# A block elimination for a 34 x 34 set of Fourier frequencies: the turned copy of U by two DMAs, apply two units ahead

## The chip, the cores and the metric

The kernel runs on one NeuronCore of a Trainium2 chip. The metric is the time of one execution on the device in microseconds (us); the value given is the median of three executions. Engines are named PE (TensorE; PEld is its weight load), ACT (ScalarE), DVE (VectorE), POOL (GpSimd) and SP (SyncE); SPq and POOLq are the queues that begin DMAs.

## The reference, cut to what matters

```python
def _L0_conv_ref(x, weight, bias):          # x: (32, 128, 32, 32) after a group norm
    xp = jnp.pad(x, ...)                     # 34 x 34
    xfft = jnp.fft.rfft2(xp, norm='ortho')   # 34 x 18 frequencies
    W = cal_wfft_ortho(weight, n, cout, cin) # one 128 x 128 complex matrix per frequency
    zfft = W @ xfft
    ...
def cal_wfft_ortho(weight, n, cout, cin):
    vfft = jnp.fft.rfft2(weight, s=(n, n), norm='ortho')
    wfft = vH @ vfft + eps * I
    ortho = I - 2.0 * (vfft @ jnp.linalg.solve(wfft, vH))
x = x + _L0_conv_ref(_gn(x), L0_conv_weight, L0_conv_bias)
```

All is float32. The costly part is a 128 x 128 complex Hermitian solve at each of 580 frequencies.

## The kernel before

The frequencies are taken four at a time, as 145 "quads". Each 128 x 128 matrix is split in two halves of 64, and each half is eliminated in blocks of 16 rows, 4 block steps to a half. A matrix half is held in 128 partitions: four quadrants of 32 partitions, a quadrant holding the real and the imaginary part of 16 rows.

The work on the solver is a list of jobs written out by hand in `order()`: form and pre build matrices, mid and final couple the halves, pivot gathers the first pivots, and a **sweep** does one block step for all quads of a group. Group 0 has 82 quads, group 1 has 63, and there are 8 sweeps of each. A sweep is cut into units of 8 quads (some of 6 or 7): 11 units for group 0, 8 for group 1, 152 in all. Each engine runs its own program through the jobs, in order, and waits on semaphores; nothing is reordered. On PE a unit has three parts:

- `apply(u)` (L1040): 32 small products with the factored pivot block `ce`; U comes out in PSUM bank 0. Its stationary operand `ce[h, ..., :, slot + t]` has 32 columns that lie 32 floats apart.
- `turn_u(u)` (L1049): one product with a constant matrix, which makes JU, U times the imaginary unit, in PSUM bank 1.
- `update(u)` (L1063): 32 products of [U, JU] with U. Stationary are 128 columns, moving 64 or 128 columns, read from 32 partitions each.

A float32 product is two instructions in the trace, so 32 products are x64. ACT copies U (L1244, `copy_u`) and JU (L1250, `copy_ju`) into the buffer `u_emb`, and gathers the pivot blocks of the next step for the unit before (L1211, `gather_next`). DVE subtracts the update from the matrices, in four instructions (L1499). The order on PE and the wait that the text below speaks of:

```python
for u in range(lo, hi):                        # L1163
    if u + 1 < hi: apply(u + 1)
    update(u)
    if u + 1 < hi: turn_u(u + 1)
# in update(u):
if u: pe.wait_ge(S["upd_copied"], 2 * u - 1)   # L1057: DVE has done two of its four for u - 1
```

`upd_bank(u, c)` is bank `2 + (4u + c) % 6`: an update takes four of six banks, so it meets the first two banks of the unit before. DVE counts `upd_copied` up after its second and fourth instruction. After a sweep, PE waits in `settle` for all of `upd_copied`. The factoring of a pivot (DVE, to `place`, L1490) runs beside the pre, mid or final job that stands between two sweeps.

## Time and profile before

| | |
|---|---|
| median of 3 runs | 2848.31 us (2847.0, 2848.31, 2858.18) |
| span of the profiled execution | 2851.4 us (its own time is given only by this span) |
| PE busy, DVE busy, ACT busy | 86%, 67%, 49% of the span |
| first and last instruction of `apply` | 541.5 and 2410.1 us |

Shares are averages over all stages. The sweeps lie between 541 and 2418 us, and each is 30 to 50 us long with the other jobs between them.

### The profile page before, as it was taken

To read this page: it belongs to the slowest core of one execution; us is meant where nothing else is said; L and a number is where in the kernel's file an instruction comes from. 1 tells how busy PE (TensorE), PEld (TensorE's weight loads), DVE (VectorE), ACT (ScalarE), POOL (GpSimd) and SP (SyncE) were. 2 spreads that over 40 slices of the span, in tenths; PEclk is the share of its full clock that TensorE was granted. 3 is DMA by queue.
4 is the path that set the end of the run, shared out by engine and by line. 5 is a ranking of instruction groups with operands and counts; after the bars stand their busy time and mean duration, and the time that the engine had idled before them with its cause. 6 is when DMAs were issued, how large, how long until landed. Compare 5 with 4: busy or idle time off the path is not lost. (4 is left out here: it accounts for less than half of the span.)

```text
span 2851.4 us, 89547 instructions
## 1 busy us (share of the span) xinstructions
PE 2466.2 (86%) x37953; PEld 2018.1 (71%) x37953; DVE 1900.5 (67%) x4779; ACT 1390.0 (49%) x3469; POOL 503.3 (18%) x872
## 2 busy tenths in 40 slices
PE   4975977999999899998987978787888888997999
PEld 4954744666566687777866767675776776987998
DVE  6852446888979768585768888897886885002444
ACT  1422422344353466665764646464565563772332
POOL 0002412121310011111111101010322221440000
PEclk7977988999999999999998989898899999997999
DMA  5274476331411283663835334361312323555874
GB/s 193 90 127 85 77 144 157 113 122 68 154 45 44 37 165 77 120 121 70 170 62 102 74 77 96 56 122 31 112 61 61 113 69 115 165 164 125 213 215 138
DMA packets 562604, 310.03 MB, mean 109 GB/s; under 512 B 484616, under 2 KB 495496, under 8 KB 561368
## 3 DMA queue, kind: packets, MB, share of 16 engines
q1 hardware_dynamic: 520896, 183.58, 30.7%
q0 software_dynamic: 41312, 120.73, 13.1%
q8 instruction: 302, 4.95, 0.7%
q14 instruction: 94, 0.77, 0.1%
HBM read 162.85 MB, written 141.30 MB: 107 GB/s over the span
## 5 line engine op out<-in xcount | busy, mean ns | idle before, releaser
L1499 DVE SCALAR_TENSOR_TENSOR arena<-arena,psum 128x512 f32<-128x512 f32 (+2 forms) x608 | 399.0, 720 | 322.5 <-PE psum L1063 322.4
L1063 PE MATMUL psum<-arena 32*128 32x128 f32 (+1 forms) x9280 | 300.4, 274 | 13.7 <-ACT arena L1250 9.7
L1040 PEld LDWEIGHTS psum<-arena 32*32 32x32 f32 x9280 | 162.0, 137 | 202.6 <-issue 201.1
L1063 PEld LDWEIGHTS psum<-arena 32*128 32x128 f32 x9280 | 279.0, 186 | 35.1 <-ACT arena L1250 20.3
L1002 PE MATMUL psum<-arena 128*32 128x256 f32 (+1 forms) x3696 | 262.7, 379 | 35.0 <-DMA arena<-plain 27.9
L1211 ACT COPY arena<-arena 32x128 f32<-32x128 f32 (+2 forms) x608 | 244.6, 402 | 92.4 <-DVE arena L1510 71.9
L1446 DVE TENSOR_TENSOR arena<-arena 128x320 f32<-128x320 f32 (+6 forms) x600 | 260.5, 485 | 8.2
L1040 PE MATMUL psum<-arena 32*32 32x64 f32 x9280 | 184.4, 231 | 89.2 <-DVEq L1491 78.7
L941 POOL COPY arena<-arena 128x512 f32<-128x512 f32 (+2 forms) x160 | 86.1, 584 | 830.1 <-ACT arena L1211 830.1
L1110 PE MATMUL psum<-arena 128*128 128x160 f32 x1160 | 198.8, 314 | 28.2 <-ACT arena L1290 28.1
L998 PE MATMUL psum<-arena 128*32 128x256 f32 (+1 forms) x2576 | 214.5, 401 | 9.9 <-DVE arena L1499 6.9
L1002 PEld LDWEIGHTS psum<-arena 128*32 128x32 f32 x3696 | 125.4, 112 | 128.5 <-issue 42.6
L1110 PEld LDWEIGHTS psum<-arena 128*128 128x128 f32 x1160 | 167.6, 193 | 63.8 <-ACT arena L1290 62.2
L1250 ACT COPY arena<-psum 128x512 f32<-128x512 f32 (+2 forms) x152 | 87.9, 578 | 248.4 <-PE psum L1049 248.4
L960 POOL DMA_DIRECT2D yhat<-arena x290 | 154.2, 538 | 299.5 <-ACT arena L1326 293.2
L1049 PE MATMUL psum<-arena 128*128 128x512 f32 (+2 forms) x304 | 176.1, 661 | 20.9 <-ACT arena L1244 20.1
L953 POOL DMA_DIRECT2D kept<-arena x145 | 103.0, 710 | 480.0 <-ACT arena L1300 454.1
L1257 ACT COPY arena<-psum 128x512 f32<-128x512 f32 x145 | 86.0, 593 | 166.3 <-PE psum L1002 162.4
L1097 PE MATMUL psum<-arena 128*128 128x96 f32 x1160 | 156.6, 280 | 10.5 <-ACT arena L1282 10.5
L1097 PEld LDWEIGHTS psum<-arena 128*128 128x128 f32 x1160 | 154.0, 198 | 15.0 <-ACT arena L1282 15.0
L1588 PE MATMUL psum<-arena 68*128 68x128 f32 x1152 | 142.9, 284 | 16.1 <-DMA arena<-yhat 16.1
L1636 DVE COPY arena<-psum 108x512 f32<-108x512 f32 (+1 forms) x96 | 57.3, 597 | 144.4 <-PE psum L1603 144.2
(126 smaller groups left out, 5020.6 us busy)
## 6 DMA issues: line engine op xcount, KB each, us to landing
blocks<-arena POOLq DMA_DIRECT2D x145, 256.0 KB, 2.3
arena<-blocks SPq DMA_DIRECT2D x290, 128.0 KB, 2.8
kept<-arena POOLq DMA_DIRECT2D x145, 256.0 KB, 3.1
arena<-kept SPq DMA_DIRECT2D x145, 256.0 KB, 3.0
xhat<-arena SPq DMA_DIRECT2D x32, 580.0 KB, 14.9
arena<-xhat SPq DMA_DIRECT2D x580, 32.0 KB, 2.6
yhat<-arena POOLq DMA_DIRECT2D x290, 64.0 KB, 2.5
arena<-x SPq DMA_DIRECT2D x8, 2048.0 KB, 9.8
```

The costliest lines, as they stand in the source:

```text
L960: pool.dma_start(yhat[r, QUAD * q:QUAD * q + QUAD, :].rearrange("c (b n) -> (c b) n", n=C), ys[:, m % 2, r, :]).then_inc(S[f"y_stored{m % ...
L998: pe.matmul(columns[quadrant(p)].rearrange("p (a k) n -> p a k n", k=m), K["ident"][:, quadrant(p)], spread(base[:, 0:m, :], 1, n), start= ...
L1002: ins = pe.matmul(columns[quadrant(p), m * a:m * a + m, :], ccoef[:, FREQ[f0 + m * a][0], :], coefs[:, 0:m, L * p:L * p + L], start=not wi ...
L1040: ins = pe.matmul(psum[0][h, L * t:L * t + L], ce[h, sj % NCE, :, slot + t], M[h, home(q) + t, c, :], start=True, stop=True)
L1049: pe.matmul(psum[1][:, 0:L * n], K["nturn"], u_emb[:, u % 2, 0:n].rearrange("p t q r m -> p (t q) r m")[:, :, 0, :], start=True, stop=True ...
L1063: ins = pe.matmul(upd_bank(u, c)[:, L * t:L * (t + m)].rearrange("p (a q m) -> p a q m", a=m, q=LB), rows.rearrange("p q r m -> p (q r m)" ...
L1097: ins = pe.matmul(psum[2][:, 3 * NB * f:3 * NB * f + 3 * NB], emb[:, m % 2, 1, f].rearrange("p q r m -> p (q r m)"), bx[:, m % 3, f, :], s ...
L1110: pe.matmul(banks[:, f // 2, f % 2, :], emb[:, m % 2, 0, f].rearrange("p q r m -> p (q r m)"), work[:, m % 2, f, 0:5 * NB], start=f % 2 == ...
L1211: ins = act.copy(dt[h, t - GROUPS[g][0], :, slot:slot + n].rearrange("p m s -> p s m"), M[h, at:at + n, c, B * piv:B * piv + B])
L1446: ins = dve.tensor_tensor(pr, spread(R[:, t, 0:rows, :, j], 3, 2 * w_), both, ALU.mult)
L1499: ins = dve.scalar_tensor_tensor(old, old, K["mask"][:, piv:piv + 1], upd_bank(u, c)[:, 0:L * n].rearrange("p (t n) -> p t n", n=L), ALU.m ...
L1588: ins = pe.matmul(S1[u % 2][:, i * 2 * H:(i + 2) * 2 * H].rearrange("p (a n) -> p a n", a=2), y_t[0:2 * N, q % 2, k, (b % BQ) * C:(b % BQ ...
```

## The change

`turn_u` leaves PE. ACT now makes two copies of U from PSUM: `copy_signed` (an activation that multiplies each partition by +1 or -1) into a buffer `signed`, and `copy_u` into the unit's buffer. ACT then begins two DMAs, SBUF to SBUF, 64 partitions x 4 runs x 512 B each (128 KB), which write the even partitions of `signed` to the odd partitions of the unit's second half and the reverse: this is JU. For that, real and imaginary rows alternate by partition, which `place` arranges with another output pattern. There are three buffers for units, two of them in `work`, and U has two PSUM banks. `apply` runs two units ahead of `update`. Within a unit the quads are now the innermost index: an operand of `update` has one column every n floats (n is 8, 7 or 6), where before its 16 or 128 columns lay side by side. SP waits for the sweeps before a later form or pre job loads its tables.

```diff
+        slot_of, landed_by, used_before = {}, {}, {}
+                turns = [0, 2, 1] if mids and mids[-1] % 2 else [0, 1, 2]
...
+        def unit(u):
+            n = sweep_units[u][1]
+            return carve_at(UNIT_AT[slot_of[u]], LB, 2, B, n)
+
+        def signed(u):
+            n = sweep_units[u][1]
+            return carve_at(SIGNED_AT[u % 2], LB, B, n)
...
+                            if before("sweep", at):
+                                sp.wait_ge(S["upd_done"], before("sweep", at))
...
-                        if u:
-                            pe.wait_ge(S["u_copied"], u)
+                        if u >= 2:
+                            pe.wait_ge(S["u_copied"], u - 1)
...
-                        pe.matmul(psum[1][:, 0:L * n], K["nturn"],
-                                  u_emb[:, u % 2, 0:n].rearrange("p t q r m -> p (t q) r m")[:, :, 0, :],
-                                  start=True, stop=True).then_inc(S["j_turned"], 1)
...
+                        pe.wait_ge(S[f"ju_in{slot_of[u]}"], landed_by[u])
                         if u:
                             pe.wait_ge(S["upd_copied"], 2 * u - 1)
                         for t in range(n):
                             for c in range(QUAD):
-                                rows = u_emb[quadrant(cls(p, c)), u % 2, t]
-
+                                rows = unit(u)[quadrant(cls(p, c)), :, :, :, t]
                                 m = 1 + (t < n - 1)
                                 ins = pe.matmul(upd_bank(u, c)[:, L * t:L * (t + m)].rearrange("p (a q m) -> p a q m", a=m, q=LB),
-                                                rows.rearrange("p q r m -> p (q r m)"), spread(real_half(rows), 1, m),
+                                                rows.rearrange("p q r m -> p (q r m)"), spread(rows[:, :, 0, :], 1, m),
                                                 start=True, stop=True)
...
                             apply(lo)
-                            turn_u(lo)
+                            apply(lo + 1)
                             for u in range(lo, hi):
-                                if u + 1 < hi:
-                                    apply(u + 1)
+                                if u + 2 < hi:
+                                    apply(u + 2)
                                 update(u)
-                                if u + 1 < hi:
-                                    turn_u(u + 1)
...
+                    def copy_signed(u):
                         act.wait_ge(S["u_done"], u + 1)
                         if u >= 2:
-                            act.wait_ge(S["upd_done"], u - 1)
...
+                            act.wait_ge(S[f"ju_in{slot_of[u - 2]}"], landed_by[u - 2])
+                        act.activation(signed(u).rearrange("p q m t -> p (q m) t"), by_column(u), ACT.Copy,
+                                       scale=K["sign"]).then_inc(S["u_signed"], 1)
+
+                    def copy_u(u):
+                        if used_before[u] >= 0:
+                            act.wait_ge(S["upd_done"], used_before[u] + 1)
+                        act.copy(unit(u)[:, :, 0, :, :], by_column(u).rearrange("p (q m) t -> p q m t", q=LB)).then_inc(S["u_copied"], 1)
+
+                    def turn_u(u):
+                        n = B * sweep_units[u][1]
+                        act.wait_ge(S["u_signed"], u + 1)
+                        if used_before[u] >= 0:
+                            act.wait_ge(S["upd_done"], used_before[u] + 1)
+                        for r in range(2):
+                            act.dma_start(every_other(UNIT_AT[slot_of[u]] + n, r, [2 * n, LB], [1, n]),
+                                         every_other(SIGNED_AT[u % 2], 1 - r, [n, LB], [1, n])).then_inc(S[f"ju_in{slot_of[u]}"], 16)
+
+                    def by_column(u):
+                        n = sweep_units[u][1]
+                        return psum[u % 2][:, 0:L * n].rearrange("p (t a) -> p a t", t=n)
...
-                            link(dve.transpose(to[:, B * piece:B * piece + B, :], pieces[:, at]))
+                            link(dve.transpose(to.rearrange("p (m r) s -> p r m s", r=2)[:, piece], pieces[:, at]))
```

The program of PE at the start of the first sweep, before the change (L1040 is `apply`, L1049 `turn_u`, L1063 `update`):

```order
L1040 MATMUL psum<-arena 32x64 [waits v_factored,v_reset,v_pre_copied,v_form_copied]
L1040 MATMUL psum<-arena 32x64 x31
L1049 MATMUL psum<-arena 128x512 [waits v_u_copied]
L1040 MATMUL psum<-arena 32x64 [waits v_u_copied,v_reset,v_factored]
L1040 MATMUL psum<-arena 32x64 x31
L1063 MATMUL psum<-arena 128x128 [waits v_ju_copied]
L1063 MATMUL psum<-arena 128x128 x27
L1063 MATMUL psum<-arena 128x64 x4
L1049 MATMUL psum<-arena 128x512 [waits v_ju_copied,v_u_copied]
L1040 MATMUL psum<-arena 32x64 [waits v_u_copied,v_reset,v_factored]
L1040 MATMUL psum<-arena 32x64 x31
L1063 MATMUL psum<-arena 128x128 [waits v_upd_copied,v_ju_copied]
```

And PE's program from the start of the same sweep with the change (L1073 is `apply`, L1087 `update`; `v_ju_in0` to `v_ju_in2` are the semaphores of the DMAs):

```order
L1073 MATMUL psum<-arena 32x64 [waits v_factored,v_reset,v_pre_copied,v_form_copied]
L1073 MATMUL psum<-arena 32x64 x31
L1073 MATMUL psum<-arena 32x64 [waits v_reset,v_factored]
L1073 MATMUL psum<-arena 32x64 x31
L1073 MATMUL psum<-arena 32x64 [waits v_u_copied,v_reset,v_factored]
L1073 MATMUL psum<-arena 32x64 x31
L1087 MATMUL psum<-arena 128x128 [waits v_ju_in0,v_u_copied]
L1087 MATMUL psum<-arena 128x128 x27
L1087 MATMUL psum<-arena 128x64 x4
L1073 MATMUL psum<-arena 32x64 [waits v_u_copied,v_reset,v_factored]
L1073 MATMUL psum<-arena 32x64 x31
L1087 MATMUL psum<-arena 128x128 [waits v_upd_copied,v_ju_in1,v_u_copied]
```

The turn is gone, three applies stand ahead of the first update, and an update waits for DMAs where it waited for ACT.

ScalarE's program a few units into the first sweep, before (L1244 `copy_u`, L1250 `copy_ju`, L1211 the gather):

```order
L1244 COPY arena<-psum 128x32x16 [waits v_upd_done,v_u_done]
L1250 COPY arena<-psum 128x32x16 [waits v_j_turned]
L1211 COPY arena<-arena 32x8x16 [waits v_taken,v_upd_copied]
L1211 COPY arena<-arena 32x8x16 x3
L1244 COPY arena<-psum 128x32x16 [waits v_upd_done,v_u_done]
L1250 COPY arena<-psum 128x32x16 [waits v_j_turned]
L1211 COPY arena<-arena 32x8x16 [waits v_taken,v_upd_copied]
L1211 COPY arena<-arena 32x8x16 x3
```

And with the change (L1265 `copy_signed`, L1271 `copy_u`, L1279 the DMAs, L1233 the gather):

```order
L1265 ACTIVATE arena<-psum,arena 128x512 [waits v_ju_in1,v_u_done]
L1271 COPY arena<-psum 128x4x128 [waits v_upd_done]
L1279 DMA arena<-arena 64x4x128 [waits v_upd_done,v_u_signed]
L1279 DMA arena<-arena 64x4x128
L1233 COPY arena<-arena 32x8x16 [waits v_taken,v_upd_copied]
L1233 COPY arena<-arena 32x8x16 x3
L1265 ACTIVATE arena<-psum,arena 128x512 [waits v_ju_in2,v_u_done]
L1271 COPY arena<-psum 128x4x128 [waits v_upd_done]
L1279 DMA arena<-arena 64x4x128 [waits v_upd_done,v_u_signed]
L1279 DMA arena<-arena 64x4x128
```

Two DMA issues have come between the copies and the gather of each unit.

## Rows read from the trace of the kernel before

**Rows 1.** The page: busy time, share and instructions of each engine.
```profile
PE 2466.2 (86%) x37953; PEld 2018.1 (71%) x37953; DVE 1900.5 (67%) x4779; ACT 1390.0 (49%) x3469; POOL 503.3 (18%) x872
```

**Rows 2.** The page's groups by line: busy us, mean ns | idle before, releaser.
```profile
L1499 DVE SCALAR_TENSOR_TENSOR arena<-arena,psum 128x512 f32<-128x512 f32 (+2 forms) x608 | 399.0, 720 | 322.5 <-PE psum L1063 322.4
L1063 PE MATMUL psum<-arena 32*128 32x128 f32 (+1 forms) x9280 | 300.4, 274 | 13.7 <-ACT arena L1250 9.7
...
L1049 PE MATMUL psum<-arena 128*128 128x512 f32 (+2 forms) x304 | 176.1, 661 | 20.9 <-ACT arena L1244 20.1
```

**Rows 3.** Timeline, one unit of the first sweep: start, us, engine, line.
```profile
561.96 1.13 PE L1049 MATMUL psum<-arena 128*128 128x512 f32 x2
...
563.02 1.16 PE L1040 MATMUL psum<-arena 32*32 32x64 f32 x64
...
563.76 1.71 ACT L1211 COPY arena<-arena 32x128 f32<-32x128 f32 x4
...
564.11 2.01 PE L1063 MATMUL psum<-arena 32*128 32x128 f32 x64
565.28 0.65 ACT L1244 COPY arena<-psum 128x512 f32<-128x512 f32 x1
...
566.05 1.13 PE L1049 MATMUL psum<-arena 128*128 128x512 f32 x2
566.19 2.72 DVE L1499 SCALAR_TENSOR_TENSOR arena<-arena,psum 128x512 f32<-128x512 f32 x4 [1.37 <-PE psum L1063]
```

**Rows 4.** Timeline, second sweep (group 0): first and last update, and what follows.
```profile
677.32 2.01 PE L1063 MATMUL psum<-arena 32*128 32x128 f32 x64
...
716.97 1.57 PE L1063 MATMUL psum<-arena 32*128 32x128 f32 x48 [0.57 <-ACT arena L1250]
718.61 2.19 DVE L1499 SCALAR_TENSOR_TENSOR arena<-arena,psum 128x384 f32<-128x384 f32 x4 [1.32 <-PE psum L1063]
...
720.85 0.64 PE L998 MATMUL psum<-arena 128*32 128x256 f32 x8 [2.31 <-DVE arena L1499]
```

**Rows 5.** Timeline, a sweep of group 1: first apply, first and last update.
```profile
1186.77 1.14 PE L1040 MATMUL psum<-arena 32*32 32x64 f32 x64 [1.17 <-issue]
...
1190.75 2.01 PE L1063 MATMUL psum<-arena 32*128 32x128 f32 x64
...
1219.08 2.01 PE L1063 MATMUL psum<-arena 32*128 32x128 f32 x56 [0.62 <-ACT arena L1250]
```

**Rows 6.** Windows before and after a PE pause; granted clock is third from last.
```profile
1991.00:1993.30 2.30, 1.73 (x49) 1.43 (x48) 1.11 (x3) 2.00 (x5) 0.00 (x0) 1.00 0.00 0
1995.60:1998.50 2.90, 2.85 (x8) 2.26 (x8) 2.73 (x9) 0.95 (x3) 1.71 (x4) 0.50 0.00 0
```

**Rows 7.** DMA issues: KB each, us to landing; SyncE's timeline, two issues.
```profile
arena<-blocks SPq DMA_DIRECT2D x290, 128.0 KB, 2.8
...
630.64 1.23 SPq L851 DMA_DIRECT2D arena<-terms  x2
```

**Rows 8.** Groups by line with shapes kept apart, ScalarE.
```profile
L1211 ACT COPY arena<-arena 32x128 f32<-32x128 f32 x480 | 198.5, 414 | 55.5 <-DVE arena L1510 48.7
...
L1244 ACT COPY arena<-psum 128x512 f32<-128x512 f32 x120 | 72.2, 602 | 129.2 <-PE psum L1040 128.5
...
L1326 ACT ACTIVATE arena<-psum,arena 128x256 f32<-128x256 f32 x145 | 68.2, 477 | 45.0 <-DMA yhat<-arena 29.8 <-PE psum L1144 15.0
...
L1211 ACT COPY arena<-arena 32x96 f32<-32x96 f32 x96 | 33.9, 353 | 30.3 <-DVE arena L1510 23.3 <-DVE arena L1499 5.9
...
L1244 ACT COPY arena<-psum 128x384 f32<-128x384 f32 x24 | 11.8, 490 | 1.0 <-PE psum L1040 0.8
```

**Rows 9.** Weight loads of three lines: ns min/median/max, first and last start.
```profile
L1040 PEld LDWEIGHTS psum<-arena x9280: 126/133/173, 541.4 to 2410.1; 32*32 32x32 f32 x198
...
L1063 PEld LDWEIGHTS psum<-arena x9280: 181/183/333, 547.8 to 2415.4; 32*128 32x128 f32 x198
...
L1142 PEld LDWEIGHTS psum<-arena x2320: 105/108/178, 2004.8 to 2574.2; 128*32 128x32 f32 x194
```

More of the change, by code:

```diff
@@ L190, in tables @@
     c["nturn"] = -turn
+    c["sign"] = np.where(i % 2 == 0, 1.0, -1.0)[:, None]
     c["avg"] = (i[:, None] // 4 == i[None] // 4) / 4.0
@@ L777, in build @@
                 jobs.append((kind, g, k, at, len(where)))
+        slot_of, landed_by, used_before = {}, {}, {}
+        for at_, (kind, g, k, lo, hi) in enumerate(jobs):
+            if kind == "sweep":
+                mids = [j[4] for j in jobs[:at_] if j[0] == "mid"]
+                turns = [0, 2, 1] if mids and mids[-1] % 2 else [0, 1, 2]
+                for u in range(lo, hi):
+                    slot = turns[(u - lo) % 3]
+                    earlier = [v for v in slot_of if slot_of[v] == slot]
+                    slot_of[u], landed_by[u] = slot, 32 * (len(earlier) + 1)
+                    used_before[u] = max(earlier, default=-1)
         def last_part(kind, g, k):
@@ L833, in build @@
         names += [f"bx_in{n}" for n in range(3)] + [f"pre_stored{n}" for n in range(NST)] + [f"tail_in{n}" for n in range(NTAIL)]
-        names += [f"part_in{n}" for n in range(4)] + [f"tile_in{n}" for n in range(6)]
+        names += [f"ju_in{n}" for n in range(3)] + [f"part_in{n}" for n in range(4)] + [f"tile_in{n}" for n in range(6)]
         with ExitStack() as es:
@@ L1237, in pivot_pieces @@
                         return out
-                    def copy_u(u):
-                        q, n, p, sj = sweep_units[u]
+                    def copy_signed(u):
                         act.wait_ge(S["u_done"], u + 1)
                         if u >= 2:
-                            act.wait_ge(S["upd_done"], u - 1)
-                        act.copy(u_emb[:, u % 2, 0:n].rearrange("p t q r m -> p (t q) r m")[:, :, 0, :],
-                                 psum[0][:, 0:L * n].rearrange("p (a m) -> p a m", m=B)).then_inc(S["u_copied"], 1)
@@ new lines, in by_column, with work_stored @@
+                    def by_column(u):
+                        n = sweep_units[u][1]
+                        return psum[u % 2][:, 0:L * n].rearrange("p (t a) -> p a t", t=n)
+                    def work_stored(at, u):
+                        done = mid_quads[0:before("mid", at)]
+                        for n in range(2):
+                            if slot_of[u] == n + 1 and done[n:]:
+                                act.wait_ge(S[f"part_stored{n}"], 16 * len([q for q in done if q % 2 == n]))
+                            if slot_of[u] == 2 and before("final", at):
+                                act.wait_ge(S[f"y_stored{n}"], 32 * len(final_quads[n:before("final", at):2]))
```

51 lines of the change are left out of this document (28 added, 23 removed).

## The prediction

> **What bounds the kernel now.** I read the page first. PE is the busiest engine, 86% of the span [rows 1], and in the groups by line the three products of a sweep are among the costliest: update and turn alone are 300 and 176 us [rows 2]. DVE's part of a sweep, 399 us, comes with 322 us of idle time that ended when an update did [rows 2]: within a sweep DVE waits for PE. Then the timeline of a sweep. From one turn's start to the next are 566.05 - 561.96 = 4.09 us, and PE's three parts follow each other without a hole: turn 1.06 us (561.96 to 563.02), apply 1.09 (to 564.11), update 1.94 (to 566.05) [rows 3]. DVE sits idle 1.37 us before each unit's four subtractions, and ACT spends 0.6 us on each of two copies of U and 1.71 on the gather, about 2.9 of the 4.09 [rows 3, 8]. So a sweep goes at PE's pace. It takes 41.2 us from the first update's start to the last one's end in group 0 (677.32 to 718.54) and 30.3 us in group 1 (1190.75 to 1221.09) [rows 4, 5]. Each sweep stands between other jobs, and PE waits for its last subtraction before it goes on [rows 4], so a shorter or longer sweep moves the end by as much.
>
> **The turn goes.** That is 1.06 us a unit off PE. Not all of it can come back. The update of a unit waits for the second of the four subtractions of the unit before. That one ends 0.14 us after PE was free (566.05 to 566.19), and then two of four: four take 2.72 at 0.72 us each [rows 2, 3], so they start 0.67 apart and the second ends after 1.39; DVE to PE takes 0.05 (718.61 + 2.19 = 720.80, PE at 720.85 [rows 4]). The gap between two updates is thus at least 0.14 + 1.39 + 0.05 = 1.58 us. Turn and apply hid it with 2.15 us; apply alone, 1.09, doesn't. If the update stays at 1.94 the unit takes 3.52 us, a gain of 0.57 and not of 1.06.
>
> **The update's operands are spread out.** This is the term on which I decide. In the new unit buffer neighbouring columns of both operands lie 8 floats apart (6 or 7 in short units). The trace has one strided operand on PE: apply loads 32 columns that lie 32 floats apart, in a median of 133 ns, where 32 columns side by side take 108 [rows 9]. The cost of a column side by side is (183 - 108) / 96 = 0.78 ns from the loads of 128 and 32 columns, and the 25 ns over 32 strided columns are again 0.78: a strided column costs twice. ACT shows such a doubling with a slope: its gather writes elements 32 floats apart and takes 414 ns for 128 and 353 for 96, 1.9 ns each; its copy of U, in runs, 602 for 512 and 490 for 384, 0.88 each [rows 8]. Against it stands that PE's 25 ns are seen at one width only and could be a fixed cost, and that no moving operand here is strided.
>
> The Trainium skill has a rule for this ("SBUF — State Buffer", section "Door 1: The DMA port swizzle"): full bandwidth wants at least two accesses to one 16-byte line, and each access to a new line pays. Columns 32 bytes apart never share a line. By that rule the update slows, by a fixed start cost it would not; rows 8 and 9 agree with the rule, as far as 32 columns and ACT's writes go.
>
> Now the update. It is 64 instructions over four quadrants side by side, 16 in a quadrant, in 1.94 us: 121 ns each, of which 128 columns at 0.78 are 100, and 21 the rest. Apply fits the same count: 1.09 / 16 = 68 ns, 64 moving columns at 0.78 are 50, and 18 the rest, its 32 strided weights hidden beside them. With strided weights at 1.56 ns a column, each instruction takes 200 + 21 = 221 ns whether or not the moving side slows too, since every product has its own weight load: 16 x 221 = 3.54 us. The bounds of this term are 1.94 (a fixed cost) and, at ACT's 1.9 ns, 16 x (243 + 21) = 4.2 us; I take 3.54, PE's own row. The unit then takes 3.54 + 1.58 = 5.12 us against 4.09.
>
> **The sweeps.** Group 0: 8 intervals of 5.12, two of 6-quad units (2.66 + 0.14 + 1.12 + 0.05 = 3.97) and the last update of 2.66 are 51.6 us against 41.2: +10.4. Group 1: 7 x 5.12 + 3.1 = 38.9 against 30.3: +8.6. Eight of each: **+152 us**. With the update at 1.94 the same sums give 35.2 and 26.3, and 8 x (6.0 + 4.0) = -80 us.
>
> **ScalarE.** copy_signed needs a scale per partition: 256 elements with one take 477 ns, and without one, by the slope, 602 - 256 x 0.88 = 377; so about 0.70 us for 512 [rows 8]. A DMA issue on SyncE takes 1.23 / 2 = 0.62 us [rows 7]. No DMA is begun by ACT here, so I bound: each unit needs 0.70 + 0.60 + 1.71 + 2 x 0.62 = 4.25 us if an issue and a copy never overlap, and 3.65 if the first issue runs beside copy_u. Both are under 5.12, so ACT costs nothing in my case; its cover is the slow update, and without that it is a rival below. Behind the issues on ACT stands the gather, for which the factoring of the next step waits, but that ends as before with the last unit.
>
> The Trainium skill ("DMA: Bandwidth & Descriptors", section "Issuing engines are not separate DMA queues") calls the time to initiate a DMA usually small beside the DMA itself. Here SyncE's 0.62 us stand against a landing of 2.8. With the issues at nothing ACT would need 3.0 us a unit and never bind.
>
> **The transfers.** A 128 KB load lands 2.8 us after its issue [rows 7]. Apply runs two units ahead, so two more applies and two gaps and updates lie between, over 6 us, against 0.70 + 0.62 + 0.62 + 2.8 = about 4.7: hidden in the steady state. At a sweep's start they aren't. Before, apply to first update takes 3.98 us [rows 5]. Now it is 1.14 + 0.05 + 0.70 + 0.05 + 0.62 + 2.8 + 0.05 = 5.4: +1.4 us, 22 us over 16 sweeps, less where a sweep starts after a wait at the low clock, so I take **+16**. PE then idles some 3 us; after a pause of 2.3 us the granted clock went from 1.00 to 0.50 (2.4 to 1.2 GHz) [rows 6]. A slow clock adds little to the strided update (its loads took at most 333 ns side by side at the low clock [rows 9], and would take 283 strided at the high one), but some 1 us a sweep to a fast one. The waits for buffers in `work` and for stores out of it find them long done, but SyncE now loads the tables of the last pre job only after the sweep before: about **+2 us**, once.
>
> **Sum.** 2851.4 + 152 + 16 + 2 = 3021 us of span; the median of the runs is 3 us below the span of the profiled execution, so **3018 us**.
>
> **The rivals.**
> - **Faster: the strided operands cost nothing** (a fixed 25 ns). The unit takes 3.52 to 3.65 us, set by DVE's half or by ACT with one issue hidden. -80 + 22 + 15 (low clock after the starts) + 2 = -41: 2807 us, from 2785 to 2833. For it: the single width; against it the match of 25 ns with 0.78 a column. Chance 0.27.
> - **ScalarE becomes the bound** (operands free, no issue hidden): 4.25 us a unit and about 0.1 of waits in the 12 sweeps that gather, 0.25 more than before over some 8 units, +24; 4 sweeps without a gather give -20; starts and tables +37. About 2889 at the full price, and no change where an issue costs 0.4 us. Chance 0.13, of which 0.08 within 0.5%.
> - **Much slower: weights and moving columns share one strided read path**, 16 x (400 + 21) = 6.7 us an update: by the same sums of the sweeps +610 us, about 3480 in all. Against it: apply's strided loads run hidden beside its moving reads. Chance 0.05.
> - **My case**, 2980 to 3080 us (update 3.2 to 4.0 us): 0.55.
>
> **How the numbers follow.** A measurement of this kernel tells 0.5%, 14 us, from no change. Faster 0.27; within 0.5%: 0.08; slower 0.05 + 0.05 + 0.55 = 0.65. The likeliest case gives 3018 us, its own range is 2980 to 3080. For 8 in 10 the range must reach the faster case, so it is 2785 to 3080; outside lie the shared path and the edges of the others, some 0.14.
>
> **What would show it.** The update's x64 taking 3.5 us instead of 1.94, with its weight loads near 280 ns instead of 183; a period near 5.1 us; DVE idle 2.4 us a unit, and ACT with slack. If the update stays at 1.9 us my step on strides is wrong: then either the gap before it is 1.6 us and ends with DVE (the faster case), or copy_signed starts late and ACT is full (the second). Each first update should start near 5.4 us after its first apply, ended by a DMA. What would break the sum besides: a landing above 5 us for SBUF to SBUF, which would put DMAs into every unit's path.

## The result and the profile after

The changed kernel takes 3118.6 us (median of 4 runs, 3094.7 to 3130.1) against 2847.7 us before (4 runs on the same chip, 2844.0 to 2858.2): a ratio of 1.092, interval 1.087 to 1.096, so 9% slower. The forecast was 3018 us with a range of 2785 to 3080: the direction was right, the size too small and the range missed. Ratios below are taken in the same way, against executions of the kernel before on the same chip; their medians were 2855.9, 2857.5 and 2855.6 us on the three other chips, so a ratio says more here than a difference of two medians.

The page of the changed kernel: groups by line, and below them a DMA issue with KB and us to landing. L1087 is `update`, L1548 the subtraction:

```profile
L1548 DVE SCALAR_TENSOR_TENSOR arena<-arena,psum 128x512 f32<-128x512 f32 (+2 forms) x608 | 398.9, 718 | 580.0 <-PE psum L1087 580.0
L1087 PE MATMUL psum<-arena 32*128 32x128 f32 (+1 forms) x9280 | 593.0, 418 | 128.1 <-DVE arena L1548 97.1
L1087 PEld LDWEIGHTS psum<-arena 32*128 32x128 f32 x9280 | 569.6, 327 | 147.4 <-issue 136.5
...
arena<-arena ACTq DMA_DIRECT2D x240, 128.0 KB, 2.7
```

The 300 us of update and 176 of turn [rows 2] became 593 us of update alone. One weight load of 128 columns takes a mean of 327 ns where the median was 183 [rows 9]. DVE's work is the same 399 us, its idle time before it grew from 322 to 580 us, and an update ended all of it.

The timeline of the changed kernel inside the first sweep (start, us, engine, line); L1073 is `apply`, L1265 `copy_signed`, L1271 `copy_u`, L1279 the two DMA issues, L1233 the gather:

```profile
559.77 4.10 PE L1087 MATMUL psum<-arena 32*128 32x128 f32 x64 [0.56 <-DVE arena L1548]
559.86 0.58 ACT L1271 COPY arena<-psum 128x512 f32<-128x512 f32 x1
559.99 1.27 ACTq L1279 DMA_DIRECT2D arena<-arena  x2
561.36 1.77 ACT L1233 COPY arena<-arena 32x128 f32<-32x128 f32 x4 [0.92 <-DVE arena L1548]
...
563.79 1.14 PE L1073 MATMUL psum<-arena 32*32 32x64 f32 x64
563.92 2.73 DVE L1548 SCALAR_TENSOR_TENSOR arena<-arena,psum 128x512 f32<-128x512 f32 x4 [2.98 <-PE psum L1087]
564.99 0.69 ACT L1265 ACTIVATE arena<-psum,arena 128x512 f32<-128x512 f32 x1 [1.87 <-PE psum L1073]
...
565.47 4.10 PE L1087 MATMUL psum<-arena 32*128 32x128 f32 x64 [0.54 <-DVE arena L1548]
...
569.50 1.93 PE L1073 MATMUL psum<-arena 32*32 32x64 f32 x64
```

The update lasts 563.79 - 559.77 = 4.02 us (1.94 in [rows 3]). The next begins at 565.47, 1.68 us later, after DVE has done two of its four subtractions ("idle before" names DVE): DVE starts 0.13 us after the update, its second instruction ends at 565.32, and 0.15 us later PE starts. The unit takes 5.70 us against 4.09. ACT is no part of this: it is idle before `copy_signed` and before the gather, and its two issues of 0.64 us each run beside `copy_u`. The transfers are 2.7 us from issue to landing and were issued two units before they are needed.

From the first update's start to the last one's end an undisturbed sweep of group 0 takes 57.7 us, where 41.2 stood in [rows 4], and one of group 1 takes 43.6 against 30.3 [rows 5]: +238 us for eight of each. As they ran, with two slower ones before the change and one after, the sixteen sum to 815 us against 583, +232 of the 277 us between the two profiled spans (3128.3 and 2851.4). The rest, 45 us: the starts of the sweeps +8 (first apply to first update, 96.5 us in sum against 88.5), the stages between the sweeps +20, of which 16 in the last four, the stage behind the last sweep +16 (451 against 436), and 1 before the first. The profiled execution is also 11 us slower than the median.

The stage behind the last sweep goes with its granted clock. Over the ten profiled executions of the two kernels and the eight whole versions below, it takes 436 to 443 us in the six where its mean clock is 0.937 or more (0.953 before the change), and 451 to 454 in the four where it is 0.924 or less (0.912 after the change, 0.77 in the middle part against 0.88). The slower kind needs no transfer: in the two executions of the kernel before with a block of products put into this stage, the rest of the stage takes 451 and 448 us, the part behind the block at 0.91. So the transfers need not be the cause there; what sets the clock, and why the last four stages between sweeps are longer, stays open.

Besides the first of each sweep one update of the change waits for its transfer, the second of the last sweep, while SyncE begins loads for the next job beside it:

```profile
2633.71 7.18 SPq L922 DMA_DIRECT2D arena<-kept  x8
...
2638.01 4.11 PE L1087 MATMUL psum<-arena 32*128 32x128 f32 x64 [3.79 <-DMA arena<-arena]
```

The start of one group 1 sweep after the change:

```profile
1133.56 2.04 PE L1073 MATMUL psum<-arena 32*32 32x64 f32 x128 [1.17 <-issue]
...
1135.47 1.28 ACTq L1279 DMA_DIRECT2D arena<-arena  x2
...
1136.18 2.14 SPq L911 DMA_DIRECT2D arena<-xhat  x2
...
1140.81 1.58 PE L1087 MATMUL psum<-arena 32*128 32x128 f32 x20 [3.61 <-issue]
```

ACT begins the first unit's transfers at 1135.47 and the update starts at 1140.81. SyncE's loads for the job that comes next are begun in between (1136.18, 2.14 us for two issues).

### The profile page after: what moved, and what is told of

Read it like the earlier page. It is cut to its first block and busy times, and to the rows that moved or that the text cites. A ratio compares the mean times of both kernels' runs of the same rounds, so it can differ in the third digit from the quotient of the medians.

```text
span 3128.3 us, 89250 instructions
## 1 busy us (share of the span) xinstructions
PE 2654.8 (85%) x37649; PEld 2349.5 (75%) x37649; DVE 1903.6 (61%) x4779; ACT 1409.6 (45%) x3469; POOL 507.9 (16%) x872
## 5 line engine op out<-in xcount | busy, mean ns | idle before, releaser
L1548 DVE SCALAR_TENSOR_TENSOR arena<-arena,psum 128x512 f32<-128x512 f32 (+2 forms) x608 | 398.9, 718 | 580.0 <-PE psum L1087 580.0
L1087 PE MATMUL psum<-arena 32*128 32x128 f32 (+1 forms) x9280 | 593.0, 418 | 128.1 <-DVE arena L1548 97.1
L1087 PEld LDWEIGHTS psum<-arena 32*128 32x128 f32 x9280 | 569.6, 327 | 147.4 <-issue 136.5
L1233 ACT COPY arena<-arena 32x128 f32<-32x128 f32 (+2 forms) x608 | 248.7, 409 | 298.0 <-DVE arena L1548 168.6
L1035 PE MATMUL psum<-arena 128*32 128x256 f32 (+1 forms) x3696 | 273.4, 377 | 37.8 <-DMA arena<-plain 29.1
L1073 PE MATMUL psum<-arena 32*32 32x64 f32 x9280 | 190.1, 239 | 94.8 <-DVEq L1540 75.8
L1265 ACT ACTIVATE arena<-psum,arena 128x512 f32<-128x512 f32 (+2 forms) x152 | 101.6, 668 | 373.8 <-PE psum L1073 330.9
L1073 PEld LDWEIGHTS psum<-arena 32*32 32x32 f32 x9280 | 170.6, 139 | 112.3 <-issue 101.0
L1031 PE MATMUL psum<-arena 128*32 128x256 f32 (+1 forms) x2576 | 227.3, 405 | 8.6 <-DVE arena L1548 6.9
L1035 PEld LDWEIGHTS psum<-arena 128*32 128x32 f32 x3696 | 146.1, 111 | 111.6 <-issue 40.0
L1134 PEld LDWEIGHTS psum<-arena 128*128 128x128 f32 x1160 | 169.5, 195 | 56.1 <-ACT arena L1331 54.4
L1121 PEld LDWEIGHTS psum<-arena 128*128 128x128 f32 x1160 | 154.1, 199 | 12.9 <-ACT arena L1323 12.9
L1637 PE MATMUL psum<-arena 68*128 68x128 f32 x1152 | 150.2, 293 | 15.8 <-DMA arena<-yhat 15.8
L1153 PEld LDWEIGHTS psum<-arena 128*128 128x128 f32 x1160 | 147.5, 206 | 16.7 <-issue 15.4
L1153 PE MATMUL psum<-arena 128*128 128x64 f32 x1160 | 157.9, 293 | 0.7 <-ACT arena L1312 0.6
```

Of the source, the lines that this page charges most:

```text
L1031: pe.matmul(columns[quadrant(p)].rearrange("p (a k) n -> p a k n", k=m), K["ident"][:, quadrant(p)], spread(base[:, 0:m, :], 1, n), start= ...
L1035: ins = pe.matmul(columns[quadrant(p), m * a:m * a + m, :], ccoef[:, FREQ[f0 + m * a][0], :], coefs[:, 0:m, L * p:L * p + L], start=not wi ...
L1073: ins = pe.matmul(psum[u % 2][h, L * t:L * t + L], ce[h, sj % NCE, :, slot + t], M[h, home(q) + t, c, :], start=True, stop=True)
L1087: ins = pe.matmul(upd_bank(u, c)[:, L * t:L * (t + m)].rearrange("p (a q m) -> p a q m", a=m, q=LB), rows.rearrange("p q r m -> p (q r m)" ...
L1121: ins = pe.matmul(psum[2][:, 3 * NB * f:3 * NB * f + 3 * NB], emb[:, m % 2, 1, f].rearrange("p q r m -> p (q r m)"), bx[:, m % 3, f, :], s ...
L1134: pe.matmul(banks[:, f // 2, f % 2, :], emb[:, m % 2, 0, f].rearrange("p q r m -> p (q r m)"), work[:, m % 2, f, 0:5 * NB], start=f % 2 == ...
```

## The experiments

Two theories. **Strides:** the columns of the update's operands, 8 floats apart, double its time, and everything else of the change is small. **Rivals:** the transfers or ScalarE's issues cost something that is hidden in the new wait (a slower landing, ports shared by DMA and PE), or the order of apply two ahead does.

**Products by themselves (`bench`, one execution).** Behind the solver of the kernel before, PE runs sets of 128 products of the update's shape: 32 partitions, 128 stationary and 128 moving columns, only the distance between columns changes.

```diff
+def columns(c, n, step, shift):
+    return bass.AP(arena, 2 * B * c * row + at + shift, [[row, 2 * B], [step, n]])
+def products(mm, w_step, m_step):
+    for n in range(4):
+        for t in range(8):
+            for c in range(QUAD):
+                mm(psum[2 + c][:, 0:2 * L]..., columns(c, 2 * L, w_step, t % w_step),
+                   spread(columns(c, L, m_step, t % m_step), 1, 2), start=True, stop=True)
```

> The kernel before, with a block of products on PE alone behind the solver: the update's shape (32 products a repeat, four repeats, 32 rows, 128 stationary and 2 x 64 moving columns, four quadrants), stationary and moving columns 1, 2, 3, 4, 8 or 16 floats apart, in turn. It reads constants and changes no result. Stride theory (the update slowed because its columns lie 8 floats apart): 1 and 1 apart take 1.9 us for 32 products; 8 and 8 take 4.0, and the doubling begins between 2 and 4 floats. If only the stationary side is slow, 8 and 1 take about 4.0 and 1 and 8 stay near 1.9. My recorded size (each strided column costs twice) gives 3.5 for 8 and 8. Rival (the update is slow because transfers and ScalarE's copies reach SBUF beside it): 8 and 8 take 1.9 to 3.5 here, where nothing else runs, and 4.0 only in the changed kernel.

Groups by line (busy us of 128 products, mean ns of one). Stationary distance 1 is L1550, 2 L1553, 3 L1556, 4 L1559, 8 L1562, with moving columns side by side:

```profile
L1562 PE MATMUL psum<-arena 32*128 32x128 f32 x256 | 15.5, 396 | 0.0
...
L1559 PE MATMUL psum<-arena 32*128 32x128 f32 x256 | 15.1, 390 | 0.0
...
L1556 PE MATMUL psum<-arena 32*128 32x128 f32 x256 | 11.4, 332 | 0.0
...
L1553 PE MATMUL psum<-arena 32*128 32x128 f32 x256 | 7.9, 276 | 0.0
...
L1550 PE MATMUL psum<-arena 32*128 32x128 f32 x256 | 7.3, 268 | 0.0
L1550 PEld LDWEIGHTS psum<-arena 32*128 32x128 f32 x256 | 7.2, 185 | 0.0
```

The same in a later stretch. Here L1565 has stationary columns 16 apart, L1568 moving columns 2 apart and L1571 4 apart, and in L1583 both are 8 apart:

```profile
L1583 PE MATMUL psum<-arena 32*128 32x128 f32 x256 | 15.5, 415 | 0.0
...
L1571 PE MATMUL psum<-arena 32*128 32x128 f32 x256 | 14.8, 402 | 0.0
...
L1565 PE MATMUL psum<-arena 32*128 32x128 f32 x256 | 14.1, 374 | 0.0
...
L1568 PE MATMUL psum<-arena 32*128 32x128 f32 x256 | 7.9, 276 | 0.0
```

A quarter of the busy time is one update of 32 products: 1.82 us side by side, 1.98 at distance 2, 2.85 at 3, 3.78 at 4, 3.87 at 8, 3.53 at 16. The moving side alone does the same: 1.98 at 2, 3.70 at 4; both sides at 8 give 3.87, no more than one. So distance 2 costs almost nothing, 4 and more doubles, and it takes only one operand (3 and 16 were tried on the stationary side alone). My forecast price, 3.5 us for 8, is missed here too, and with no other engine at work. The granted clock was 1.00 (2.4 GHz) in the windows of this stretch. The Trainium skill's rule of two accesses to a 16-byte line ("SBUF — State Buffer", section "Door 1: The DMA port swizzle") has a step between 2 and 4 floats, and the rows agree with it for both sides of a product. The same note says that 4 fp32 can be strided for free; taken as a distance this does not hold here, where 4 apart took 3.78 us against 1.82. That 8 apart costs more than 16 apart is not in the rule.

**The change with columns closer (`e1_step1`, `e1_step2`, `e1_step4`, 4 executions each).** The unit buffer is cut into pieces of STEP quads, so columns lie STEP floats apart; the runs of the transfers are then 64 x STEP bytes long, 512 in the change itself.

```diff
+        STEP = 1        # 2, 4
-            return carve_at(UNIT_AT[slot_of[u]], LB, 2, B, n)
+            return carve_at(UNIT_AT[slot_of[u]], -(-n // STEP), LB, 2, B, STEP)
...
-                                rows = unit(u)[quadrant(cls(p, c)), :, :, :, t]
+                                rows = unit(u)[quadrant(cls(p, c)), t // STEP, :, :, :, t % STEP]
...
-                            act.dma_start(every_other(UNIT_AT[slot_of[u]] + n, r, [2 * n, LB], [1, n]),
+                            act.dma_start(every_other(UNIT_AT[slot_of[u]] + n, r, [2 * n, runs], [1, n]),
```

> The change, with a unit's columns side by side (1 float apart, as before it) and so transfers in runs of 64 B instead of 512 B. Stride theory: the update is back at 1.94 us; the gap before it is 1.7 us, or ScalarE sets the pace with its 3.8 us of work a unit; the period is 3.7 to 4.0 us instead of 5.7, and the time 2810 to 2870 us, if 2048 runs a transfer land within 5 us. Rival (traffic beside PE): the update stays above 3 us and the time above 2950. Rival (the two-ahead order and ScalarE's issues are what costs): the period stays above 5 us.

> The change with columns 2 floats apart (two quads interleaved) and transfers in runs of 128 B. Stride theory with a line of 16 bytes: two columns share a line, the update stays at 1.94 us, time 2810 to 2870. If every stride above 1 costs, the update takes 4.0 us and the time stays near 3110. Traffic rival: above 2950.

> The change with columns 4 floats apart and transfers in runs of 256 B. Stride theory with a line of 16 bytes: each column is in a line of its own, the update takes 4.0 us as in the change, time within 1% of 3118. If the cost grows with the distance, it lies between that of 2 and of 8 floats. Traffic rival: no difference to the change either, but then none at 1 and 2 floats apart too.

| distance | time, us | ratio to before | interval | shortest period, us | landing, us |
|---|---|---|---|---|---|
| 8 (the change) | 3118.6 | 1.092 | 1.087 to 1.096 | 5.70 | 2.7 |
| 4 | 3113.5 | 1.091 | 1.089 to 1.093 | 5.63 | 2.8 |
| 2 | 2901.2 | 1.017 | 1.013 to 1.021 | 3.83 | 3.1 |
| 1 | 2939.4 | 1.029 | 1.027 to 1.031 | 3.63 | 4.3 |

At distance 2 and 1 the update is back at 2.17 and 1.95 us and the period is below the 4.09 before. Of the 9.2% that the change costs, 7.5 come back by distance 2. Yet no version is faster than before, side by side is worse than distance 2, and my 2810 to 2870 us for both were missed. The timeline of the version with distance 1 shows the best case and what spoils it (L1088 is `update`, L1074 `apply`, L1266 `copy_signed`, L1280 the issues, L1234 the gather):

```profile
1228.67 2.02 PE L1088 MATMUL psum<-arena 32*128 32x128 f32 x64 [0.55 <-DVE arena L1549]
1229.77 0.69 ACT L1266 ACTIVATE arena<-psum,arena 128x512 f32<-128x512 f32 x1
...
1230.48 1.73 ACTq L1280 DMA_DIRECT2D arena<-arena  x2
1230.62 1.00 PEld L1074 LDWEIGHTS psum<-arena 32*32 32x32 f32 x64
...
1232.30 2.02 PE L1088 MATMUL psum<-arena 32*128 32x128 f32 x64 [0.54 <-DVE arena L1549]
1232.31 1.70 ACT L1234 COPY arena<-arena 32x128 f32<-32x128 f32 x4 [1.34 <-DVE arena L1549]
1234.02 0.69 ACT L1266 ACTIVATE arena<-psum,arena 128x512 f32<-128x512 f32 x1
```

PE's period is 1232.30 - 1228.67 = 3.63 us: update 1.95, then 1.68 of gap that ends with DVE. But the two issues take 1.73 us instead of 1.27, and 3.1 and 3.4 at the start of this same sweep. From one `copy_signed` to the next ACT needs 4.25 us (1229.77 to 1234.02), with the gather at 1232.31 behind the issues. So ScalarE has no slack left, as my second rival had it, and transfers come late: besides the first of each sweep 22 updates wait for theirs, 39 us in sum. That is not all that lengthens the intervals, though. Of the 88 between units of 8 quads, the first of each sweep left out, 41 are over 3.95 us, and 22 of these hold a pause of over 0.15 us in which PE waits for nothing that the profile names; I come back to it with the last pair.

**Distance and width (`bench2`, one execution).** Because the update had come out above my price, the same products with other distances and with fewer stationary columns. The diff is against `bench`; 128 moving columns go with the wide loads.

```diff
-                def products(mm, w_step, m_step):
+                def products(mm, width, w_step, moving):
+                                h = quadrant(c) if width == 32 else slice(0, width)
+                                mm(psum[2 + c][h, 0:L], columns(c, width, w_step, t), columns(c, L, 1, 0), start=True, stop=True)
```

> The kernel before, with products on PE alone behind the solver, reading constants, to find why 32 columns understated the price: 128 stationary columns 1, 8, 32 and 16 floats apart, then 32 columns 1, 4, 8, 16 and 32 apart (apply's shape), then 64 and 96 columns 8 apart. If the distance matters, 32 floats apart is cheaper than 8 at the same width: 128 columns take about 280 ns a load at 32 apart and 332 at 8. If the width matters (a first stretch of columns is free), 32 columns cost 25 ns more at any distance from 4 up, and 128 cost 147 more at any. With one price a column of 0.78 ns, which I had assumed, 128 columns would add 100 ns; the first bench has 147 at 8 floats and 121 at 16.

Groups by line: 128 stationary columns 8 apart (L1553) and 32 apart (L1556); then 32 columns, 8 (L1568), 32 (L1574) and 1 (L1562) apart:

```profile
L1553 PE MATMUL psum<-arena 32*128 32x128 f32 x256 | 15.4, 397 | 0.0
L1553 PEld LDWEIGHTS psum<-arena 32*128 32x128 f32 x256 | 15.4, 330 | 0.0
L1556 PE MATMUL psum<-arena 32*128 32x128 f32 x256 | 14.3, 378 | 0.0
L1556 PEld LDWEIGHTS psum<-arena 32*128 32x128 f32 x256 | 14.2, 308 | 0.0
...
L1568 PEld LDWEIGHTS psum<-arena 32*32 32x32 f32 x256 | 4.2, 142 | 2.8 <-issue 2.8
...
L1574 PEld LDWEIGHTS psum<-arena 32*32 32x32 f32 x256 | 3.8, 129 | 3.4 <-issue 3.4
...
L1562 PEld LDWEIGHTS psum<-arena 32*32 32x32 f32 x256 | 3.7, 104 | 0.5 <-issue 0.4
```

Here is the price that I had read: 32 columns that lie 32 floats apart cost 129 - 104 = 25 ns more, just the 25 ns of [rows 9]. It is true for that shape only. At 128 columns the same distance costs 308 - 185 = 123 ns, 0.96 ns a column instead of 0.78, and distance 8 costs 330 - 185 = 145, 1.13 a column (185 is the load side by side in `bench`). The distance counts at 32 columns too: 8 apart costs 142 - 104 = 38 ns. For an update: 3.57 us at distance 32, and 3.85 at 8.

**The kernel before with spread columns (`e2_before_spread`, 4 executions).** No DMA, the turn stays on PE, one apply ahead; only U and JU are stored with the quads innermost.

```diff
-                                rows = u_emb[quadrant(cls(p, c)), u % 2, t]
+                                rows = unit(u)[quadrant(cls(p, c)), :, :, :, t]
...
-                                                rows.rearrange("p q r m -> p (q r m)"), spread(real_half(rows), 1, m),
+                                                rows.rearrange("p q r m -> p (q r m)"), spread(rows[:, :, 0, :], 1, m),
```

> The kernel before with one part of the change alone: a unit's columns lie 8 floats apart. The turn stays on PE, there is no transfer, apply runs one unit ahead. Stride theory: the update takes 4.0 us, turn and apply 2.15, the period is 6.2 us, which gives +20 us a sweep of group 0 and +16 of group 1, about 3150 us, slower than the change itself by the 0.5 us a unit that removing the turn gives back. Traffic rival: the update stays near 2 us and the time at 2850.

3132.0 us, ratio 1.093 (1.089 to 1.098): as slow as the whole change. Its timeline (L1064 `update`, L1050 the turn, L1041 `apply`):

```profile
558.71 4.09 PE L1064 MATMUL psum<-arena 32*128 32x128 f32 x64
...
562.73 1.13 PE L1050 MATMUL psum<-arena 128*128 128x512 f32 x2
...
563.79 1.13 PE L1041 MATMUL psum<-arena 32*32 32x64 f32 x64
...
564.85 4.09 PE L1064 MATMUL psum<-arena 32*128 32x128 f32 x64
```

The update takes 4.02 us with no transfer anywhere, and the three parts on PE follow each other again: 4.02 + 1.06 + 1.06 = 6.14 us a unit. This tells the theories apart: the layout alone makes a loss as large as the whole, and an update is no faster without transfers beside it (4.02 us in both kernels). The rest of the change brings a unit from 6.14 to 5.70 us and the sweeps from 855 to 815 us in sum, but the whole does not gain: in the profiled executions 8 us go at the starts, 20 in the stages between the sweeps and 15 in the stage behind the last (437 and 451 us), and the ratios, 1.093 and 1.092, do not differ.

**SyncE begins the transfers (`e6_sync_step8`, `e7_sync_step2`, 4 and 10 executions).** The first is the change with its issues moved to SyncE, the second the same with distance 2.

```diff
+                    def turn_u(u):                      # in SyncE's program
+                        sp.wait_ge(S["u_signed"], u + 1)
+                        ...
+                            sp.dma_start(...)
...
+                        elif kind == "sweep":
+                            for u in range(lo, hi):
+                                turn_u(u)
...
-                                    turn_u(u + 2)       # in ScalarE's
```

> The change with its transfers begun by SyncE instead of ScalarE. In the change ScalarE has slack (period 5.70 us, its own work 3.8), so the steady state stays at 5.70 and the update at 4.0. SyncE now loads the next job's parts only after the sweep's transfers, so a sweep's first transfers no longer queue behind them: first update 5.4 us after the first apply instead of 7 in group 1, about -10 us, less what the later loads cost: 3095 to 3125 us. Rival (ScalarE's issues are what made the change slow): below 3000.

> Columns 2 floats apart and the transfers begun by SyncE. With step 2 and ScalarE the period was 3.84 us, which is ScalarE's own work. Without the two issues ScalarE needs 3.0 us, and the gap behind DVE's second subtraction (1.7) with the update (1.95) sets 3.65 us: -0.2 us for each of some 120 units, and shorter starts, together -25 to -45 us on 2901: 2855 to 2875 us, no better than the kernel before. Rival (transfers' landing sets the pace at step 2): the period stays at 3.84.

With distance 8: 3102.9 us, ratio 1.082 (1.077 to 1.087). The period stays at 5.70; shorter are the starts of the first four sweeps of group 1:

```profile
1131.68 2.04 PE L1085 MATMUL psum<-arena 32*32 32x64 f32 x128 [1.24 <-issue]
...
1133.58 10.48 SPq L878 DMA_DIRECT2D arena<-arena  x7
...
1137.51 4.10 PE L1099 MATMUL psum<-arena 32*128 32x128 f32 x64 [2.20 <-issue]
```

From first apply to first update it is 5.83 us here, against 7.25 after the change (1133.56 to 1140.81): SyncE is still busy with these issues, seven of them in a row, and has not begun the loads for the next job that stood between the transfers and the update after the change. I take the earlier start to come from that, though engine and order changed together. The landing is 2.4 us instead of 2.7.

With distance 2: 2872.9 us, ratio 1.006 (1.003 to 1.009). ScalarE's issues thus cost 28 us where the update is fast (2901.2 to 2872.9), but not in the period: it stays 3.84 us with them gone, and it is update 2.17 plus gap 1.67, the same DVE gap. What they cost shows in the last sweep. In the profiled execution of `e1_step2` two single intervals of 10.2 and 11.4 us stand there, which make 13 of the 19 us by which its sweeps and starts are longer than here, and PE waits in both for a transfer (L1280 are ScalarE's issues):

```profile
2421.41 3.59 PE L1088 MATMUL psum<-arena 32*128 32x128 f32 x64 [5.57 <-DMA arena<-arena]
...
2422.12 7.78 ACTq L1280 DMA_DIRECT2D arena<-arena  x2
```

SyncE begins loads for the next job in the same stretch, and two issues hold ScalarE for 7.78 us. With SyncE issuing, these loads stand behind the transfers, and no update waits for its transfer but the first of a sweep. So ACT does not set the period at distance 2, as I had supposed ahead of this run. The start of one of its sweeps (L1086 `apply`, L1100 `update`):

```profile
2300.85 0.90 PE L1086 MATMUL psum<-arena 32*32 32x64 f32 x44 [0.85 <-issue]
...
2302.42 3.65 PE L1100 MATMUL psum<-arena 32*128 32x128 f32 x64 [0.67 <-ACT arena L1284]
...
2307.66 2.24 PE L1100 MATMUL psum<-arena 32*128 32x128 f32 x64 [0.52 <-DVE arena L1549]
...
2311.50 1.78 PE L1100 MATMUL psum<-arena 32*128 32x128 f32 x46 [0.53 <-DVE arena L1549]
```

PE pauses 0.67 us before an update that takes 3.57 us (2302.42 to 2305.99). The granted clock was 1.00 until 2302.4, 0.53 and then 0.50 (1.2 GHz) in the update: at the start PE had been busy 0.90 of 1.55 us, and 1.02 of the 2.30 before. The first interval is 5.24 us instead of 3.84; the next update takes 2.17 at 1.00.

**The first unit turned on PE (`e8_first_on_pe_step2`, `e9_first_on_pe_step1`, 12 executions each).** If the starts were what was left, they had to go. The constant for this product takes the place of another one; for that, one of ACT's copies in the final jobs now multiplies by -1 (279 ns in the median instead of 268, 145 times).

```diff
+                    def turn_first(u):
+                        pe.wait_ge(S["u_copied"], u + 1)
+                        pe.matmul(turn_bank(u), K["pairs"], unit(u)[:, :, :, 0]..., start=True, stop=True)...
...
                             apply(lo)
                             apply(lo + 1)
+                            turn_first(lo)
...
-                            for u in range(lo, hi):     # SyncE
+                            for u in range(lo + 1, hi):
```

> The turned copy by DMA with columns 2 floats apart and SyncE issuing, as in the run before it, but the first unit of each sweep is turned by a product on PE, as before. My theory: what was left over against the kernel before was the start of each sweep, where PE idles about 2.2 us and then runs its first update at a low clock (3.65 to 3.69 us instead of 2.17, first interval 4.8 to 5.5). With the first turn on PE the start is about 4.5 us again and the first interval 3.84, so group 0's sweeps take about 38.5 us (41.2 before the change) and the whole about 2830 us (2815 to 2850), about 1% below the kernel before. Rival: the second unit's transfer is not there in time or another wait holds the first interval above 5 us; then 2865 us or more.

> The same with adjacent columns (64-byte runs in the transfers, about 4.3 us from issue to landing instead of 3.1). If a lead of two units covers a landing of 4.3 us, the period is 1.94 + 1.68 = 3.63 us and the whole 2810 to 2850 us. If it does not, some intervals are 4 us and more, as they were with ScalarE issuing, and the whole is 2860 to 2930 us.

2855.7 us against 2855.6, ratio 0.999 (0.996 to 1.002), and 2865.7 us, 1.004 (1.002 to 1.006). My forecast of 2830 us for the first failed; the second is in the 2860 to 2930 us that I had for intervals of 4 us and more. Half of what I had for the first came true: five of eight group 1 sweeps start within 4.2 us, first intervals are 3.85 to 4.9, and from first apply to last update the 16 sweeps take 652 us in sum against 671 before (9 of the 19 us are two slower sweeps in that execution of the kernel before). But the spans of the two profiled executions differ by 4 us only (2847.5 and 2851.4): the stages between and behind the sweeps are 15 us longer, and the medians do not differ. And many intervals inside the sweeps are 4.0 to 4.5 us. In the version with distance 1, 57 of the 88 intervals between units of 8 quads, the first of each sweep left out, are over 3.95 us. One of them (L1120 `update`, L1098 `apply`):

```profile
1331.09 0.72 PE L1120 MATMUL psum<-arena 32*128 32x128 f32 x15 [0.55 <-DVE arena L1577]
...
1332.35 1.67 PE L1120 MATMUL psum<-arena 32*128 32x128 f32 x49 [0.54 <-issue]
...
1333.94 1.14 PE L1098 MATMUL psum<-arena 32*32 32x64 f32 x64
```

The update is cut in two, 15 and 49 rows with 0.54 us between them in which PE waits for nothing that the profile shows, at a granted clock of 1.00; it ends 2.85 us after its start instead of 1.95. DVE and the next unit are late by as much. In the next unit the cut comes after 14 rows, and in three units of the first sweep after 41, 40 and 39: it moves by one row a unit, as a count of instructions would, and belongs to no operand.

The DMA packets of the trace say what comes in just before. One DMA queue carries instructions; the page has its packets and MB:

```profile
q8 instruction: 299, 4.90, 0.7%
```

These are packets of 16 KB, in a sweep about one for each unit. Of the pauses inside these sweeps over 0.15 us in which PE waits for nothing named, 55 of 55 end 1.2 to 1.6 us after such a packet has ended, though only a tenth of the sweeps' time lies that far behind one. In `e8_first_on_pe_step2` it is 22 of 22, and in the kernel before 2 of 2, both in its slow last sweep. So in these pauses PE waits, as far as the packets show, for its own instructions. They sum to 37 us with distance 1, 10 with distance 2 and 3 before the change, and 41 of the 57 long intervals with distance 1 hold one. The packets themselves take no longer (0.96 us in the median, before the change too). Why they come late was not tried: the transfers may hold them up (SyncE begins them without a break in this stretch), or a unit of 3.63 us asks for them sooner than one of 4.09.

## Why the prediction was wrong

- **What bounds the sweep** held: PE's update and then DVE's half, with ACT idle before it.
- **The turn goes, the gap stays** held: I had 1.58 us from the end of one update to the next, it is 1.68. The difference is the hand-over from DVE to PE, 0.15 us where I took 0.05 from another line. Over 120 units those 0.10 are 12 us.
- **The update's operands are spread out** is the step that failed, in its size. Its mechanism is shown by the spread version of the kernel before (update 4.02 us, total as slow as the change) and by the versions with columns closer. The price was 3.54 us for an update and it measured 4.02 (a weight load 332 ns in the median, where I had 280). The difference, by the bench: I took the price of a column from loads of 32 columns that lie 32 floats apart and multiplied it by 128. At that distance 128 columns give 3.57 us by themselves, so the multiplication was nearly right there, but only because my remainder of 21 ns already held what the bench lacks: in the kernel an update side by side takes 1.94, in the bench 1.82. The distance of 8 instead of 32 adds 0.28 us, the moving side no more than 0.02, and the surroundings in the kernel 0.15 (3.87 to 4.02; it is there without transfers too, and side by side it is 0.12). With the 0.03 from 3.54 to 3.57 these are the 0.48 us. With 4.02 and 1.68 for my 3.54 and 1.58 the same sums give 8 x 5.70 + 2 x 4.39 + 3.0 = 57.4 us a sweep of group 0 and 7 x 5.70 + 3.6 = 43.5 of group 1, +235 us instead of +152, and 3101 us for the whole.
- **The range** stopped at an update of 4.0 us, though my bound was 4.2 (ACT's 1.9 ns a column). That bound was right to keep, and the range of the likeliest case should have reached to it: by the same sums 4.2 us gives 6.8 us more in each sweep of group 0 and 5.2 in each of group 1, so 3018 + 96 = 3114 us.
- **ScalarE costs nothing** held for the change, by the cover that I named, the slow update. The issues overlap `copy_u`. With the cover gone its issues cost 28 us at distance 2, none of it in the period; in the profiled executions 13 of 19 us are in the last sweep. At distance 1 ACT needs 4.25 us a unit, and 22 updates wait for late transfers, 39 us; in `e9_first_on_pe_step1`, where SyncE issues and the first unit is turned on PE, it is 9 updates and 12 us.
- **The transfers are hidden** held in the steady state (landing 2.7 us, foreseen 2.8), but for one update of the last sweep that waits 3.8 us beside SyncE's loads. At the starts I had +16 us and it is +8: five are 5.4 to 5.7 us as I had them, the others between 4.8 and 8.4, those of the first four group 1 sweeps about 7; but eleven of the sixteen were over 5 us before, too.
- **The stages outside the sweeps** were put at +2 us. In the profiled execution they are 37 us longer (1 before, 20 between and 16 behind the sweeps), as large a term as is missing from the 3101 us; the part behind goes with its granted clock, the rest has no cause that I can show.
- **The faster case** was priced with operands that cost nothing, 2807 us. The version with distance 1 has those operands and shows that case's period, 3.63 us (I had 3.52 to 3.65), yet takes 2939 us: with the 64-byte runs that this layout leaves, issues and landing are dearer, and PE pauses for its instructions.

Where the gain of the idea went: 1.06 us of turn leave PE, of which 0.46 can be seen in a period (4.09 to 3.63), the rest being DVE's half. In the 120 units that is at most 55 us; the best version keeps 19 us of it in the sweeps of its profiled execution, 9 of them owed to the two slow sweeps before, and none in the median.

## What to carry to other kernels

Before a layout is changed so that a DMA gets longer runs, look at how far apart it puts the columns that PE reads: 2 floats were nearly free, 3 cost half again, 4 and more doubled a product of 128 by 128 float32 columns, whichever side had them. A price read from one shape and distance was too low for another here; take the range up to the dearest neighbouring row. And when a product is taken off PE, first find what waits behind it: here the next wait stood 0.46 us further on, and behind that one stood PE's own instructions.

## What the runs showed of the hardware that I had not expected

- A product with one spread operand costs as much as with two: 3.70 to 3.87 us for 32 products with stationary, moving or both 4 to 8 floats apart. Distances of 16 and 32 are cheaper than 8 (3.53 and 3.57 against 3.87).
- A spread update does not depend on the granted clock: from its start to the next apply it takes 4.04 us at 0.50 (at 548.15 in the changed kernel) and 4.02 at 1.00 (at 1836.60). Side by side it goes from 1.95 us to 3.62 (at 1219.73 in `e1_step1`). The apply took 1.93 us at 0.50 instead of 1.14.
- An SBUF to SBUF transfer of 128 KB lands after 2.7 us with runs of 512 bytes (2.4 when SyncE begins it), 3.1 with 128 and 4.3 with 64. One issue holds ScalarE for 0.62, 0.68 and 0.95 us in the median. Beside SyncE's loads in the last sweep two of them held it for 1.4, 7.8 and 16.4 us.
- PE can be held up by its own instructions: 55 of 55 unnamed pauses in the sweeps of `e9_first_on_pe_step1` ended 1.2 to 1.6 us after a 16 KB packet of the instruction queue, 0.23 to 1.17 us each for eight in ten.
